# The back transpose of a pair's result, moved into the score product of the step

## What is computed

```
x = layernorm(x + gated_sum(x, W, a, adj))          # 1: sums over neighbours
x = layernorm(x + gat(x, adj, Wh, bh, Wo, ...))     # 2: 4 heads, then a second layer
x = layernorm(x + add_att(x, adj, W2, a2, 0.01))    # 3
x = layernorm(x + add_att(x, adj, W3, a3, 0.2))     # 4

gat_layer(h):  scores = h @ h.T; scores = where(mask, scores, -1e16)
               out = softmax(scores) @ h + b
add_att:       e = leaky(left_i + right_j); e = where(mask, e, NEG)
               out = softmax(e) @ h
```

## Time and profile before

| | |
|---|---|
| median of 3 runs | 6510.92 us (6500.03 to 6516.5) |
| profiled execution | 6511.56 us, its span 6509.8 us |
| mean granted TensorE clock | 0.942 |
| PE busy | 5744.7 us, 88% |
| weight loads (PEld) busy | 4654.5 us, 71% |
| DVE busy | 4424.1 us, 68% |
| ACT busy | 3901.8 us, 60% |
| POOL busy | 1599.2 us, 25% |
| L887, the back transpose | 448 times, 131.6 us |

### The profile page before, as it was taken

One profiled execution on the slowest core, in us unless ns is written; L12 is line 12 of the kernel. 1 busy time (PEld: TensorE's weight loads), 2 busy tenths in 40 slices (PEclk: granted clock), 3 DMA queues, 4 the chain that ended last, 5 costly groups with the idle time before them and its releaser, 6 DMA issues.

```text
span 6509.8 us, 163090 instructions
## 1 busy us (share of the span) xinstructions
PE 5744.7 (88%) x52064; PEld 4654.5 (71%) x52064; DVE 4424.1 (68%) x7928; ACT 3901.8 (60%) x5701; POOL 1599.2 (25%) x1239
## 2 busy tenths in 40 slices
PE   7689898998989888998989989898889989899866
PEld 4268676886768777786768867687777867688655
DVE  4756476766766676766767667766767677676765
ACT  1056457666666656666576666666566675766655
POOL 0100014023230413104140231304131041402354
PEclk9889899999999999999989999999999999899988
DMA  4200000000000000000000000000000000000000
GB/s 137 64 5 2 1 5 2 2 2 9 5 2 2 2 11 2 2 2 4 10 2 2 2 9 5 2 2 3 11 2 2 2 4 9 2 2 2 8 1 4
DMA packets 99234, 55.58 MB, mean 9 GB/s; under 512 B 89424, under 2 KB 92752, under 8 KB 98384
## 3 DMA queue, kind: packets, MB, share of 16 engines
q1 hardware_dynamic: 60496, 34.71, 1.9%
q10 hardware_dynamic: 37888, 9.97, 0.7%
HBM read 35.75 MB, written 8.91 MB: 7 GB/s over the span
## 4 chain that ended last, share of the span: by engine, by line
PE 67%; issue 9%; DVE 9%; ACT 5%; DVEq 3%; POOL 1%; ACTq 0%; DMA 0%; SPq 0%; POOLq 0%
PE tp L878 23%; PE po L898 23%; PE pss L869 7%; PE pss L868 7%; DVE rows L1172 3%; DVEq L237 3%; ACT pss L1039 2%; DVE pt L1184 2%; ACT rows L1060 2%; PE px L829 2%; PE px L825 1%; PE tp L887 1%; PE px L843 1%; PE px L835 1%; DVE tmp L254 1%
## 5 line engine op out<-in xcount | busy, mean ns | idle before, releaser
L878 PE MATMUL tp<-ident,rows 128*128 128x128 f32 x14336 | 2054.5, 285 | 181.6 <-DVE pt L1184 89.7
L1184 DVE COPY pt<-tp 128x512 f32<-128x512 f32 x2048 | 1336.5, 686 | 1287.7 <-PE tp L878 1272.5
L878 PEld LDWEIGHTS tp<-ident,rows 128*128 128x128 f32 x14336 | 1609.7, 144 | 592.0 <-issue 554.9
L1060 ACT ACTIVATE rows<-rows,nm 128x2048 f32<-128x2048 f32 x896 | 1797.5, 2006 | 265.4 <-DVE nm L1172 257.5
L898 PE MATMUL po<-pt,hn 128*64 128x128 f32 x28672 | 1887.0, 288 | 0.5 <-DVE pt L1184 0.2
L898 PEld LDWEIGHTS po<-pt,hn 128*64 128x64 f32 x28672 | 1667.8, 145 | 164.7 <-issue 164.7
L707 POOL TENSOR_TENSOR rows<-sr,mask 128x2048 f32<-128x2048 f32 x256 | 1046.4, 4088 | 697.3 <-PE tp L878 679.2
L1012 ACT COPY pt<-tp 128x512 f32<-128x512 f32 x1536 | 850.7, 589 | 449.1 <-PE tp L878 429.2
L868 PE MATMUL pss<-ha 128*128 128x512 f32 x2560 | 1067.8, 417 | 24.6 <-issue 15.3
L869 PE MATMUL pss<-ha,hb 128*128 128x512 f32 x2560 | 1015.3, 397 | 0.0
L1172 DVE CUSTOM_DVE_ANT_0 rows<-pss,mask,nm 128x1024 f32<-128x1024 f32 x640 | 821.7, 1284 | 202.6 <-issue 201.4
(11 more groups left out here) (102 smaller groups left out, 3375.0 us busy)
## 6 DMA issues: line engine op xcount, KB each, us to landing
adjb<-in_adj SPq DMA_DIRECT2D x32, 512.0 KB, 4.6
xin<-x SPq DMA_DIRECT2D x9, 512.0 KB, 4.2
xb<-in_x ACTq DMA_DIRECT2D x16, 256.0 KB, 3.4
x<-t ACTq DMA_DIRECT2D x16, 256.0 KB, 2.7
xb<-x SPq DMA_DIRECT2D x8, 512.0 KB, 4.2
out<-xb SPq DMA_DIRECT2D x32, 128.0 KB, 2.0
xtp<-in_xt SPq DMA_DIRECT2D x12, 256.0 KB, 6.6
ab<-in_a ACTq DMA_DIRECT2D x16, 64.0 KB, 3.3
```

Of the source, the lines that this page charges most:

```text
L878: last = nc.tensor.transpose(tp[row.bank[q]][:, r * P:(r + 1) * P], rows[:, row.slot, jb * P:(jb + 1) * P], ident[:])
L1060: nc.scalar.activation(rows[:, row.slot, :], rows[:, row.slot, :], ACT.Exp, scale=-1.0, bias=nm[:, row.t, 1:2], accum_out=rs[:, row.t:row. ...
L1184: nc.vector.tensor_copy(pt[:, CH * q:CH * (q + 1), row.k % SLOTS, :], tp[row.bank[q]][:].rearrange("p (j n) -> p j n", n=P)).then_inc(pt_d ...
```

## The change

The back transpose of a step that has a score product is issued inside it: after the two matmuls of the third bank (c = 2) and before the two of the fourth, whose last one announces the second half. In steps without a score product (additive rows, gaps) it stays where it was.

```diff
-            def dot_products(row):
+            def dot_products(row, back):
...
                         nc.tensor.matmul(pss[:, cols], ha[i][:, rows_t], moving, start=True, stop=False)
                         last = nc.tensor.matmul(pss[:, cols], hb[i][:, rows_t], moving, start=False, stop=True)
+                        if c == NC // 2 and back:
+                            turn_back(back)
                     last.then_inc(scores_ready, 1)
...
                     if row and row.gat:
-                        dot_products(row)
-                    if segment.back(s):
+                        dot_products(row, segment.back(s))
+                    elif segment.back(s):
                         turn_back(segment.back(s))
```

## The result

| | before | changed |
|---|---|---|
| median of 8 runs each | 6517.82 us (6500.03 to 6531.91) | 6538.51 us (6528.62 to 6552.84) |
| ratio, 95% interval | | 1.0035 [1.002, 1.0051] |
| profiled execution: time, span | 6511.56, 6509.8 | 6547.02, 6545.2 |
| its mean granted clock | 0.942 | 0.938 |

The change makes the kernel slower by about 21 us of medians, just over the 0.3% that can be told from nothing. The forecast was 6526, "same" being a little likelier than "slower". One of the six executions of experiment 2 took 14920.65 us; it stands apart from all others of this document and isn't in that experiment's numbers.

A forecast was written before the change was run, and what follows sets the result against it. TensorE (PE), busy 88% of the span, was taken to bound the kernel. From 6511.56 us, −26.1 + 34.3 + 1 + 5.6 = +14.8 gave 6526.4, stated as 6526; range 6488 to 6556, with "same" between 6491.4 and 6530.4.

The forecast's parts named there:

- G: Saving in free steps (no task between): 0.29 us each before the second turn, −26.1 us over loop and prologue.
- Rival 4: Free steps lack the tenth of slack for `ot`, so half of G goes: 13 us more, 6539; chance 0.06.
- Rival 3: Weights behind the moved transpose load in the open: 0.05 us times 316, 16 us more, 6542; chance 0.03.
- L: Cost where PE waits for DVE or `ot`: 4.7 us per iteration, +34.3 with prologue, 1 more for epilogue.
- Rival 1: DVE sets the length of every step with a wait; L vanishes and G stays: 6486 us; chance 0.13.
- the 0.28: Wait per step where `ot` comes just in time: slack 0.18 us, place 0.46 earlier; 1.4 us per iteration.
- The clock: Drops to 1.2 GHz behind lengthened long waits: one drop of 1.6 us in two iterations, +5.6 us.
- Rival 2: Longer waits tip the clock nearly each time: 34 us in place of 5.6, 6555 us; chance 0.28.

The follow-up runs named there:

- experiment 2: Kernel before, with the back transpose moved inside the product only in steps that have a PE task: 6555.5 us, ratio 1.006.
- experiment 5: Kernel before, with one transpose of a turn issued twice in every step of head 3 in the loop, as plain PE work: ratio 1.0034.
- experiment 1: Kernel before, with the back transpose moved inside the product only in steps without a PE task: 6498.0 us, ratio 0.9974.
- experiment 3: Kernel before, with the back transpose moved inside the product only where an `hn` task follows a `proj` task in the step before: ratio 1.0035.
- experiment 6: Kernel before, back transpose at its old place but into its own bank part, `po[:, 128:256]`, waiting for `ot` alone: 6403.3 us, ratio 0.9829.
- experiment 7: Kernel before, with both edits: back transpose into its own bank part (`po`) and issued inside the product: 6392.8 us, ratio 0.9819.
- experiment 8: The kernel of experiment 6, plus a wait at the transpose for the copy its old bank would have needed: 6466.7 us, ratio 0.9928 to before.

## Why the prediction was right, and where it wasn't

**G (−26.1) held, nearly.** The hole is gone, a pair of head 3 takes 11.41 us for 11.40 forecast, head 3 fell by 1.8 for 1.7 (six steps of 0.29), and the prologue by 3.9 where −5.6 and +1.4 make −4.2. The count was one short: the table of tasks gives 13 free steps per iteration, not 12, which would be another 2.0 us in seven, and the epilogue's 3 were left out. Rival 4 (no tenth of slack for `ot` in free steps) is out: `ot` to transpose's end is 0.81 there in the changed kernel, above the floor of 0.69. Rival 3 (open weights) is out by the row at 5199.53. The Trainium skill's rule on row groups (TensorE: Matmul & The Clock Gate, Part 3, "The mechanism"), by which that load would lie open, does not agree with that row. The same section also names a background buffer for weights as a second way for a load to go ahead; no run here tells whether this load used it.

**L (+34.3 and 1) held in kind, and in size within some 10 us.** Head 2: four projection steps of +0.28 and two free ones of −0.29 make +0.5; it grew by 0.5, each time. The other three GAT units should share the rest, 4.7 − 2.9 + 1.7 − 0.5 = 3.0 us: `GAT2`, head 0 and head 1 grew by 2.3, 0.8 and 1.4 in the sixth iteration, 4.5 in all, each at the same mean granted clock as before; so L came out up to 1.5 us per iteration dearer than said in these units, some 10 us in seven. Rival 1 (VectorE takes L up) is out: the 62 waits grew by 0.46 each, and experiment 2 shows their price. The model behind the 0.28, a fixed distance of 0.69, was right for this kernel but not a constant: 0.25 of it belongs to the second wait.

**The clock (+5.6) is the term that failed**, by size and by place. I had looked for it behind the three next longest waits for VectorE, two in `GAT2` and one in head 0. These three grew as forecast, and none tipped the clock:

```profile
4615.41 0.30 PE L889 MATMUL tp<-ident,ot 128*128 128x128 f32 x1 [1.27 <-DVE pt L1186]
...
4704.98 0.30 PE L889 MATMUL tp<-ident,ot 128*128 128x128 f32 x1 [1.47 <-DVE pt L1186]
...
4762.90 0.30 PE L889 MATMUL tp<-ident,ot 128*128 128x128 f32 x1 [1.55 <-DVE pt L1186]
```

The granted clock is 1.00 in the 4 us behind each, though two of them are longer than the 1.38 us behind which it was 0.50 before. The forecast had also passed over the wait of 1.44 us for `ot` in `GAT2` (listed in the earlier trace rows), behind which the kernel before does fall to 0.50.

What grew is the time at 1.2 GHz elsewhere. The clock records of the two profiled executions, summed over the seven iterations, have 187.7 us of it in `ADD2` before and 215.0 after, 32.0 and 50.1 in `GAT2`, and hardly more in `ADD1` (228.7 and 232.1) and head 0 (20.5 and 23.9). `ADD2` is 17.4 us longer over these iterations and `GAT2` 18.3; half of the added time at 1.2 GHz, 14 and 9 us, is an estimate of the clock's part in each. In `GAT2` the rest is L. Over the whole executions it is 752 and 807 us at 1.2 GHz, half of the difference is 27, and the spans differ by 35.4: 8 are left where G and L sum to +9.2.

That is one pair of executions. A second estimate uses all of them. In the three series of the kernel before, with 19, 11 and 23 executions, a mean granted clock lower by 0.001 goes with 5.5, 5.7 and 5.1 us more. The changed kernel's mean over 8 executions is 0.9389; that of before is 0.942 in these series (the clocks of the executions that it was compared with were recorded for one only). 0.0031 by 5.4 is some 17 us. The means of the 8 runs each differ by 23, so 6 are left for everything else. The same sum leaves 6 of its 22 us for experiment 5, where head 3 grew by 6.2; 36 of its 40 for experiment 2, where L was put at 35; and −32 from the −17 of experiment 1, where G was put at −26. This is a fit between executions, with a clock given to three digits; I take both estimates, 17 and 27 us, for the order of the term where I had put 5.6. Rival 2's size (34) was thus too large, its sign right: it spoke of drops behind the lengthened waits, and behind those three none came.

Against the 6510.92 us of the first runs, 14.8 were forecast and 21 to 23 measured side by side; 6538.5 lies in the range, 8 us above the edge at 6530.4 from which I called it slower. That the range held it is partly luck: it reached up to rival 2's time, for drops that didn't come there, and the clock's share came by a way that the forecast didn't name.

**What stays open** is why `ADD2` is longer in nearly every variant (and `ADD1` in none, by the table), also where its instructions and the unit ahead of it are as before, as in experiment 3. `ADD2` took 118.3 to 120.5 us in the first four iterations of the profiled execution of before and 115.5 in the last three, with no change of code between them. Only the faster kernels of experiments 6 and 7 had `ADD2` units below 114 us. No run here tells what decides where the stretches at 1.2 GHz fall.

## What to carry to other kernels

When a transfer or a small instruction shares a buffer with the main stream, ask first what the wait ahead of it holds up, not where it stands: moving it earlier closed a 0.29 us hole in some steps and put 0.46 us of matmuls behind a late wait in others, while a buffer part of its own removed both and gave 1.7 to 1.8%. In a kernel that runs partly at half clock, cost an edit by the units that stay at full clock, and expect a gain or loss of some 10 to 20 us from the clock alone: 6 us of plain work cost 22.

## What the hardware showed that I had not expected

A stand-alone wait (here a wait and the increment of a semaphore, as `stand_alone_wait` issues them; the share of each isn't shown) that is already satisfied still costs PE 0.25 us when it stands behind a late one: 0.69 us against 0.44 from `ot`'s end to the transpose's end, and 0.24 more behind VectorE once the order is turned. Not behind an early one: head 2 and head 3 are the same to 0.1 us with the extra wait of experiment 8 and without it, in experiment 6.

The length of a wait doesn't tell whether PE falls to 1.2 GHz behind it. In the kernel before it was at 0.50 after a wait of 1.38 us and after 2.49 us of idleness; in the changed one waits of 1.47 and 1.55 us and 2.79 us of idleness left it at 1.00. And executions of one kernel differ by 30 us in step with their mean granted clock, 0.939 to 0.944.
